# Second attention: probabilities scaled ahead of the value products, and products on quarters of the array that come out turned

## What is computed

```python
qh = (q @ Wq).reshape(b, l, HEADS, HEAD_DIM).transpose(0, 2, 1, 3)
kh = (kv @ Wk).reshape(b, s, HEADS, HEAD_DIM).transpose(0, 2, 1, 3)
vh = (kv @ Wv).reshape(b, s, HEADS, HEAD_DIM).transpose(0, 2, 1, 3)
qh = rms_norm(qh, q_norm_w)
kh = rms_norm(kh, k_norm_w)
mask = (jnp.arange(s, dtype=jnp.int32)[None, :] < x_seqlens[:, None])[:, None, None, :]
scores = jnp.einsum('bhld,bhsd->bhls', qh, kh) * (1.0 / np.sqrt(HEAD_DIM))
scores = jnp.where(mask, scores, NEG_INF)
attn = jax.nn.softmax(scores, axis=-1)
o = jnp.einsum('bhls,bhsd->bhld', attn, vh)
o = o.transpose(0, 2, 1, 3).reshape(b, l, HEADS * HEAD_DIM)
return o @ Wo
```

## Time and profile before

| | us |
|---|---|
| median of 3 runs | 2436.03 |
| lowest and highest of the 3 | 2432.83, 2439.78 |
| the profiled execution | 2432.44 |
| its span, first to last instruction | 2430.6 |
| TensorE busy in it (matmuls) | 2107.6 |
| VectorE, ScalarE, GpSimd busy | 1658.2, 882.9, 614.3 |

### The profile page before, as it was taken

How to read it: one execution, slowest core, us unless ns; L and a number is a source line. 1 busy time by engine, 2 the same in 40 slices (tenths; PEclk the granted TensorE clock), 3 DMA queues, 4 the chain that set the end, 5 groups by cost and what they waited for, 6 DMA issues and landing times. The chain is left out here.

```text
span 2430.6 us, 38588 instructions
## 1 busy us (share of the span) xinstructions
PE 2107.6 (87%) x12427; PEld 1162.5 (48%) x12427; DVE 1658.2 (68%) x3378; ACT 882.9 (36%) x1559; POOL 614.3 (25%) x833
## 2 busy tenths in 40 slices
PE   4759999999899879999999989789988999768965
PEld 2634444444444436666666644335553444324531
DVE  4857776676776657777777669757755666536668
ACT  4522112202201136666666644213332222223335
POOL 4641110110110135555555432321200000021201
PEclk8569999999999889999999999879979999979975
DMA  3403203212230331111111100000004323210001
GB/s 102 147 1 71 54 20 68 53 42 45 53 69 18 71 110 35 33 35 34 30 35 32 30 0 1 1 11 12 11 5 108 106 66 98 54 28 13 12 4 35
DMA packets 131759, 106.41 MB, mean 44 GB/s; under 512 B 95400, under 2 KB 113704, under 8 KB 127152
## 3 DMA queue, kind: packets, MB, share of 16 engines
q1 hardware_dynamic: 131632, 104.84, 17.4%
HBM read 80.85 MB, written 2.97 MB: 34 GB/s over the span
## 5 line engine op out<-in xcount | busy, mean ns | idle before, releaser
L1026 PE MATMUL l0f_acc<-l0f_z,w_all 128*128 128x512 f32 x512 | 236.5, 625 | 22.8 <-DVE l0f_z L1250 22.8
L918 POOL TENSOR_TENSOR l0f_v<-l0f_val,l0f_top 64x256 f32<-64x256 f32 x128 | 78.4, 613 | 521.0 <-DVE l0f_val L1210 513.4
L972 PE MATMUL l0f_work<-w_all,l0f_xs 128*128 128x512 f32 x384 | 190.2, 619 | 9.5 <-DVE l0f_val L1205 8.2
L1026 PEld LDWEIGHTS l0f_acc<-l0f_z,w_all 128*128 128x128 f32 x512 | 101.8, 200 | 157.1 <-issue 130.0
L241 POOL TENSOR_SCALAR var_eps<-mean_var 128x4 f32<-128x4 f32 (+1 forms) x64 | 14.6, 229 | 545.9 <-DVE mean_var L225 544.1
L2288 PE MATMUL a_score<-keys_by_head,a_qT 128*64 128x512 f32 x512 | 143.4, 642 | 9.1 <-DMA keys_by_head<-w_all 9.1
L1210 DVE COPY_PREDICATED l0f_val<-l0f_oh,l0f_work 128x512 f32<-128x512 int32 x160 | 117.0, 731 | 49.4 <-PE l0f_work L972 31.7
L2780 DVE TENSOR_TENSOR l2f_hu<-l2f_act_g,l2f_pu 128x512 f32<-128x512 f32 x104 | 71.2, 684 | 68.6 <-ACT l2f_act_g L2706 67.3
L2706 ACT ACTIVATE l2f_act_g<-l2f_pg 128x512 f32<-128x512 f32 x104 | 61.5, 594 | 149.3 <-PE l2f_pu L2647 137.4
L2655 PE MATMUL l2f_acc<-l2f_hid,w_all 128*128 128x512 f32 x208 | 107.4, 598 | 9.6 <-DVE l2f_hid L2786 9.6
L1710 DVE TENSOR_REDUCE l1x_ms_k<-l1x_sq_k 128x8 f32<-128x512 f32 x64 | 43.9, 686 | 102.6 <-ACT l1x_sq_k L1596 102.5
(11 more groups left out here) (363 smaller groups left out, 4841.3 us busy)
## 6 DMA issues: line engine op xcount, KB each, us to landing
l0f_first_mask<-onehots SPq DMA_DIRECT2D x32, 512.0 KB, 5.7
w_all<-onehots SPq DMA_DIRECT2D x32, 512.0 KB, 11.1
l1x_v<-l1x_vr SPq DMA_DIRECT2D x256, 64.0 KB, 2.1
w_all<-combination SPq DMA_DIRECT2D x40, 256.0 KB, 5.2
w_all<-in_weights SPq DMA_DIRECT2D x1, 4640.0 KB, 17.1
l0x_m_b<-running_max SPq DMA_DIRECT2D x16, 256.0 KB, 4.7
keys_by_head<-w_all SPq DMA_DIRECT2D x256, 8.0 KB
keys_by_head<-ctxT_all SPq DMA_DIRECT2D x256, 8.0 KB
```

The costliest lines, as they stand in the source:

```text
L918: nc.gpsimd.tensor_tensor(v2[a * SEQ:(a + 1) * SEQ, t % 2, b, :, a, :], val[r, t % 2, :, :].rearrange("p (c a) k -> p c a k", a=2)[:, :, a ...
L972: nc.tensor.matmul(value_banks[e % 3][:, :], xs[:, t * P:(t + 1) * P], ve[:, e, :], start=True, stop=True).then_inc(ve_done, 1)
L1026: nc.tensor.matmul(acc[:, :], oe[:, n % E, n // E, :], z[:, n % Z, :], start=(n == 0), stop=(n == C * E - 1)).then_inc(acc_done, 1)
```

## The change

Five things move together, all in `l1_xattn`:

- The probabilities are scaled before they are multiplied: `scale_probs` on VectorE takes the place of `scale_out`, right behind `totals`, and writes them in place. `prob` has two halves, used in turn; `og` is gone.
- Turned probabilities go to the bank turn1 and stand one slot later (lag 3), right behind `project_q`; their copy probT is ScalarE's second step. `turn_k` waits for that copy.
- The value products stand one slot later too, behind `project_v` and ahead of `turn_k`. They are done in quarters of the array: v2 (64 keys by 64 features of one head, without zeros now) is the stationary operand and probT the moving one, so the result is the output already turned (features by tokens). 16 matmuls of 64 columns replace 8 of 128.
- `turn_out` is gone. oT is copied from po as soon as the products are done; that copy stands ahead of the kb copies on ScalarE.
- On VectorE `mean_k` moves behind `normalise_q`. GpSimd no longer clears v2, and SyncE no longer waits for that.

```diff
@@ l1_xattn
-        v2 = sb("v2", [P, 2, 2, C, 2, HD])
+        v2 = sb("v2", [P, 2, 2, C, HD])
-        diff, prob = sb("diff", [P, HU, SEQ]), sb("prob", [P, HU, SEQ])
+        diff, prob = sb("diff", [P, HU, SEQ]), sb("prob", [P, 2, HU, SEQ])
...
-                sp.wait_ge(v2_zero, count(2))
...
-                nc.gpsimd.memset(v2[:, :, :, :, :, :], 0.0).then_inc(v2_zero, 1)
...
                 def turn_k(n):
                     pe.wait_ge(nm_k_done, count(n + 1))
                     after(pe, kT_ready, n)
-                    after(pe, oT_ready, n - 2)
+                    pe.wait_ge(pT_ready, count(max(n - 1, 0) if isinstance(n, int) else n - 1))
...
-                def turn_probs(n):
-                    pe.wait_ge(exp_done, count(n + 1))
-                    pe.wait_ge(qT_ready, count(at_most(n + 2, U * GROUPS)))
+                def turn_probs(g, j):
+                    n = U * g + j
+                    pe.wait_ge(prob_ready, count(n + 1))
+                    pe.wait_ge(kT_ready, count(at_most(n + 2, U * GROUPS)))
                     after(pe, pT_ready, n)
...
                     pe.wait_ge(v_loaded[j % 2], 64 * (4 * g + j // 2 + 1))
-                    after(pe, og_ready, n)
+                    after(pe, oT_ready, n)
+                    pe.sem_inc(may_multiply, 1)
                     for c in range(C):
                         for b in range(2):
-                            q = slice(b * SEQ, (b + 1) * SEQ)
-                            ins = nc.tensor.matmul(po[q, c * P:(c + 1) * P], probT[:, c, q],
-                                                   v2[:, j % 2, b, c, :, :].rearrange("p a e -> p (a e)"),
-                                                   start=True, stop=True)
+                            for a in range(2):
+                                r = slice(a * SEQ, (a + 1) * SEQ)
+                                q = slice(b * SEQ, (b + 1) * SEQ)
+                                ins = nc.tensor.matmul(po[r, c * P + b * SEQ:c * P + (b + 1) * SEQ], v2[r, j % 2, b, c, :],
+                                                       probT[r, c, q], start=True, stop=True)
                     ins.then_inc(pv_done, 1)
-
-                def turn_out(n):
...
-                    act.wait_ge(o_turned, count(n + 1))
+                    act.wait_ge(pv_done, count(n + 1))
...
-                def scale_out(n):
-                    dve.wait_ge(pv_done, count(n + 1))
+                def scale_probs(g, j):
+                    n = U * g + j
                     dve.wait_ge(inv_done, count(n + 1))
-                    after(dve, o_turned, n)
-                    nc.vector.tensor_tensor(og[:, :, :], heads(po[:, :]), bcast(inv[:, :], 2, HD), ALU.mult)\
-                        .then_inc(og_ready, 1)
+                    nc.vector.tensor_tensor(prob[:, j % 2, :, :], prob[:, j % 2, :, :], bcast(inv[:, :], 2, SEQ), ALU.mult)\
+                        .then_inc(prob_ready, 1)
```

More of the change, by code:

```diff
@@ L1450, in turn_q @@
                     after(pe, qT_ready, n)
-                    after(pe, pT_ready, n - 1)
                     for c in range(C):
@@ L1497, in values @@
                     pe.wait_ge(v_loaded[j % 2], 64 * (4 * g + j // 2 + 1))
-                    after(pe, og_ready, n)
+                    after(pe, oT_ready, n)
+                    pe.sem_inc(may_multiply, 1)
                     for c in range(C):
                         for b in range(2):
-                            q = slice(b * SEQ, (b + 1) * SEQ)
-                            ins = nc.tensor.matmul(po[q, c * P:(c + 1) * P], probT[:, c, q],
-                                                   v2[:, j % 2, b, c, :, :].rearrange("p a e -> p (a e)"),
-                                                   start=True, stop=True)
-                    ins.then_inc(pv_done, 1)
-                def turn_out(n):
-                    pe.wait_ge(og_ready, count(n + 1))
-                    pe.wait_ge(kT_ready, count(at_most(n + 3, U * GROUPS)))
-                    after(pe, oT_ready, n)
-                    for c in range(C):
-                        ins = nc.tensor.transpose(turn1[:, c * P:(c + 1) * P],
-                                                  og[:, 2 * c:2 * c + 2, :].rearrange("p a e -> p (a e)"),
-                                                  core.const("ident"))
-                    ins.then_inc(o_turned, 1)
+                            for a in range(2):
[3 more added lines that the diff above has]
+                                                       probT[r, c, q], start=True, stop=True)
+                    ins.then_inc(pv_done, 1)
                 def project_out(g, j):
@@ L1536, in slot @@
                         project_q(g, j)
+                    h, i = lagging(g, j, 3)
+                    if live(h):
+                        turn_probs(h, i)
                     h, i = lagging(g, j, 1)
@@ L1545, in slot @@
                         project_v(g, j)
+                    h, i = lagging(g, j, 3)
+                    if live(h):
+                        values(h, i)
                     h, i = lagging(g, j, 1)
@@ L1571, in slot @@
                         scores(h, i)
-                    h, i = lagging(g, j, 2)
-                    if live(h):
-                        values(h, i)
                 for g in range(2):
@@ L1629, in copy_pT @@
                     after(act, pv_done, n)
-                    nc.scalar.activation(probT[:, :, :], turn0[:, :].rearrange("p (c q) -> p c q", c=C), ACT.Copy)\
+                    nc.scalar.activation(probT[:, :, :], turn1[:, :].rearrange("p (c q) -> p c q", c=C), ACT.Copy)\
                         .then_inc(pT_ready, 1)
@@ L1638, in copy_oT @@
                     nc.scalar.activation(oT[:, j // 4, h * C:(h + 1) * C, tok],
-                                         turn1[:, :].rearrange("p (c q) -> p c q", c=C), ACT.Copy).then_inc(oT_ready, 1)
+                                         po[:, :].rearrange("p (c q) -> p c q", c=C), ACT.Copy).then_inc(oT_ready, 1)
                 def copy_yT(pair):
@@ L1650, in slot @@
                         square_q(U * g + j)
+                    h, i = lagging(g, j, 3)
+                    if live(h):
+                        copy_pT(U * h + i)
+                    h, i = lagging(g, j, 2)
+                    if live(h):
+                        exp(h, i)
                     h, i = lagging(g, j, 1)
@@ L1653, in slot @@
                         copy_qT(U * h + i)
-                    h, i = lagging(g, j, 2)
+                    if live(g):
+                        copy_v(g, j)
+                    h, i = lagging(g, j, 3)
                     if live(h):
-                        exp(U * h + i)
+                        copy_oT(h, i)
                     h, i = lagging(g, j, 1)
```

48 lines of the change are left out of this document (16 added, 32 removed).

## The result

The changed kernel takes 2459.51 us (median of 4 runs, 2458.03 to 2460.59); the kernel before, on the same chip, 2434.88 (4 runs, 2432.83 to 2439.78). The ratio is 1.0093, 95% interval 1.0078 to 1.0108, so the change costs about 23 us (the two medians lie 24.6 apart). The profiled execution took 2460.01, its span is 2457.9. Forecast was 2453, range 2437 to 2478.

A forecast was written before the change was run, and what follows sets the result against it. The prediction took TensorE's stream to bound the kernel, with the kb copies ending a wait in each slot of the second attention. Three slots at +0.30 and one at +0.14 gave 1.04, times 16 about 17 us: 2453, range 2437 to 2478.

The forecast's parts named there:

- Item 1, 2: Second attention: turned outputs' 0.46 us leaves; mask waits for kb until 2.12 after k's turning (T), TensorE idling about 0.8.
- Item 3: Turned probabilities move out of the kb copies' shadow to behind the q projection: 0.44 us a slot, now paid in full.
- Item 4: Value products, 32 instructions on quarters between v projection and k's turning: 1.04 us, with 0.96 as the lower end.
- Item 5: Changing the array's split twice more: scores +0.10 us, v projection +0.10, the transposes behind the products +0.06.
- Item 6: ScalarE's output copy right ahead of the kb copies just fits; if not, up to 0.1 us a slot on top.
- The step that was short: Mask start behind the kb copies: put where turned outputs had started, 2.12 us after k's turning.
- Sum: Loop between k's turnings: 7.35 us against 7.05, +0.30; slot of 7.21 +0.14; four slots 1.04, 16 fours +16.6.
- (a): Rival: TensorE's work decides, not the kb copies; 0.52 us a slot less, 33 us less, 2403; chance 0.08.
- (b): Rival: no change, ways in and out of the split cost nothing; +0.04 a slot, +2 us, 2438; chance 0.12.
- (c): Rival: quarters writing one PSUM bank take turns; a pair 0.108 us, +50 us more, 2503; chance 0.10.
- (d): Rival: TensorE's clock falls to 0.97 over the stage because it idles; +16 us more, 2469; chance 0.06.
- Item 7: VectorE's swapped multiplication and later mean of k priced at nothing; normalised k at T+6.2, 0.1 more after the change.

The follow-up runs named there:

- Experiment 1: Changed kernel with the mask matmul ahead of the waits for turned q and kb: 2437.99 us, ratio 1.0016 to the kernel before.
- experiment 2: Changed kernel with probabilities turned behind the k projection again: 2448.87 us, ratio 1.0058 to the kernel before; with the mask ahead of the wait too, 2440.21, 1.0029.
- experiment 7: Kernel before with only its value products put on quarters of the array, still behind the scores: 2447.79 us, ratio 1.0053.
- Experiment 5: Changed kernel with the mask's address a constant of the slot, not worked out from the loop's counter: 2457.13 us, ratio 1.0091 to the kernel before.
- experiment 6: Changed kernel with the 16 value products of the upper quarter first, then the 16 of the lower: 2508.16 us, ratio 1.0301 to the kernel before.
- experiment 8: Kernel before with the mask matmul moved ahead of the turned outputs, out of the waits for q and kb: 2424.53 us, ratio 0.9966.
- last version of experiment 3: Changed kernel with mask ahead of kb's wait, probabilities turned behind k projection, additions to x behind scaling, xn turned behind the probabilities: 2426.51 us, ratio 0.9960 to before.
- early split of experiment 4: Changed kernel with the second kb copy on VectorE behind the totals, and additions to x behind the scaling: 2470.93 us, ratio 1.0142 to the kernel before.

## Why the prediction was right, and where it was short

The mechanism was right. In the slot of 7.05 the turned outputs leave the path (-0.46), and the turned probabilities, which lay in the shadow of the kb copies, come into it (+0.44). What is left is the array's split: T to mask +0.05, scores +0.10, v projection +0.09, products +0.10, together +0.32. Experiment 1 shows that this wait rules the slot, by moving only the mask across it; experiment 2 gives the turned probabilities back in three slots of four, and experiment 7 has the price of the quarters alone. The time is 6.5 us over the forecast of 2453 and inside its range.

- **Item 1, 2 (turned outputs leave, the mask waits for kb).** T+2.12 to 2.18 was forecast, 2.17 is measured where the address is not in the way, with an idle time of 0.66 or 0.75 where 0.8 was said.
- **Item 3 (turned probabilities, 0.44 in the open).** Measured 0.44 from 1114.98 to 1115.42, with no wait. Experiment 2 shows that putting them back isn't worth 0.44 everywhere: the one slot in four where VectorE adds to x loses 0.71.
- **Item 4 (value products).** 1.04 was taken, 1.08 measured. The rows of the narrow attention have 18 columns, and a pair follows the other every 0.058 in both: the 64 columns cost nothing in the pace. The 0.04 lie at the ends, 0.03 behind the first pair and 0.01 at the way out. 2.6 us in all.
- **Item 5 (ways in and out of the split).** As said: scores to q projection 1.02, v projection 0.95 where 0.96 was forecast, four turnings behind the products 0.49 where four took 0.43 or 0.44 before. Experiment 7 shows 0.10 for the way in apart from all moves, and 0.10 for the products themselves.
- **Item 6 (output copy ahead of the kb copies: "it just fits, up to 0.1 a slot on top").** It does fit: kb starts at T+0.69 and T+0.70. The second row has no idle time in front (1118.59), so the record shows nothing to spare.
- **The step that was short.** "They start when the turned outputs did, at T+2.12": what stands between the end of kb and the mask was taken as the same as for the turned outputs. Those have fixed addresses; the mask's comes from the loop's counter. In five of eight slots of the loop the computation stands behind the wait and costs 0.10 to 0.11: 25 slots, 2.6 us. Experiment 5 takes this away (2.7 between the q projections).
- **Sum.** Forecast 1.04 for four slots, 16.6 us in all. Four slots without the address computation show 1.14 (9.10, 7.37, 7.37, 9.10 against 31.8), 1.6 us more over 16 fours; the address computation is 2.6. The stage grew by 23.1, so 2.2 are left, at its ends, which were not priced.
- **Rivals.** (a), TensorE's work decides: wrong, with idle time ahead of the mask in every slot, and experiment 1. (b), no change: wrong, experiment 7 (by the prediction's own items it would even have come to +0.00, not +2 us: three slots at +0.04 and one at 0.14 - 0.26). (c), the quarters take turns: wrong, experiment 6, and a pair takes 1.08 / 16 = 0.068 with the way out where turns need 0.108. The rule of the Trainium skill, "TensorEngine Tiling (Array Packing)", Restrictions and Gotchas, that different row tiles can't access the same PSUM bank simultaneously, doesn't hold for these quarters: the two of a diagonal, on different partitions of one bank, share the array. (d), the clock falls: wrong for this change, 1.00 from 900 to 1380; the idle times of 0.4 to 0.8 ahead of the masks did not lower it.
- **Item 7 (VectorE, nothing).** Right for the change as it was made: no wait for it stands in TensorE's queue. The T+6.2 for the normalised k was misread: the earlier trace rows start it at 1112.93, so it was done at T+6.64, with 0.7 to spare. In the changed kernel, where no output is scaled ahead of it, it is done at T+6.25, and 1.1 is left. The misreading touched no term of the sum. VectorE was the reason why six of the expectations behind it were too good: the 1 us a slot is there only as long as TensorE itself is late.

The 4 us behind the stage in the profiled execution go with the clock: it stood at 0.50 for 11 us more there, by an estimate 5.5 us of work at full speed. In the kernel before with the mask moved (experiment 8) the part behind the stage took 1022 us with 196 us at 0.50, in the last version of experiment 3 1032 us with 223. Why the clock was lower in one execution than in another is open. By the ratio (23 us) against the stage (23.1) the 4 us aren't in the median; by the two medians (24.6 apart) up to 1.5 us of them could be.

## What to carry to other kernels

Find the wait that ends each slot first, and count what the change moves across it: work ahead of it is free up to the shadow's length, work behind it is paid, and taking work out ahead of it gains nothing. The cheapest edit is then often to move a step without that dependency (a mask, a bias) ahead of the wait; one such move was worth 0.3% in the kernel before and 0.8% in the changed one. When a wait is shortened, look at once at the engine that comes next: here VectorE, with a busy share of 71% in the changed kernel, took back part or all of the gain in six of twelve runs, most of it by a step that stood too late in its order within the slot.

## What the runs showed of the hardware

- An address worked out from a loop counter can stand behind a semaphore's wait as a register operation of its own, and then costs 0.1 us on the critical path: kb's end to the mask took 0.19 to 0.21 in the 25 slots with it, and 0.10 in those without, and 0.10 in experiment 5, where the address is fixed. In the other 15 slots of the loop the wait stood on the weight load and nothing was lost; what decides between the two is not shown.
- Two float32 products on diagonal quarters of the array that write one PSUM bank run together: 32 instructions of 64 columns in 1.08 us when they alternate (0.058 a pair), 1.83 when they don't (0.058 each).
- A change of the array's split costs 0.09 to 0.10 us, by starts of single instructions: last pair of scores to first pair of products on quarters 0.21 where a pair of halves followed after 0.11 (experiment 7); last pair on quarters to the turning of k 0.155 where pairs are 0.058 apart (the changed kernel); the mask 0.31 ahead of the scores and 0.22 ahead of work on the whole array; the last turned outputs 0.20 ahead of the scores and 0.11 apart from each other (experiment 8).
- Idle times of 0.4 to 0.8 us in every slot left TensorE's clock at 1.00. Of twelve idle times of 2.25 to 2.28 us in one run (the early split of experiment 4), four went with a granted clock of 0.50, that is 1.2 GHz, for 3.4 us, and eight did not: the same k projection took 1.70 in the first case and 0.86 in the second.
